# Two buffers for the normalised tile, and a chunk normalised one turn earlier in the halo loop of a state-space and ternary-FFN kernel

## The reference, cut to what matters

```python
u = jnp.einsum('bld,nd->bln', _layernorm(x), W_in)      # 64 states
h = h * Abar + u_t * Bbar                               # scan over the tokens
x = x + jnp.einsum('bln,dn->bld', h * C, W_out)
...
def _quant_weight(w): s = mean(|w|); wq = clip(round(w / s), -1, 1) * s
def _quant_act(x): scale = 127 / max|x| per row; xq = round(x * scale) / scale
h = gelu(_quant_act(_layernorm(x)) @ _quant_weight(w1).T)   # 1024 -> 4096
x = x + _quant_act(h) @ _quant_weight(w2).T                 # 4096 -> 1024
```

## Time and profile before

| | us |
|---|---|
| runs before | 2258.49, 2260.24 (median), 2263.87 |
| the profiled execution | 2268.22 |
| its span, slowest core (core 4) | 2266.7 |
| spans of the 8 cores | 2242.1 to 2266.7 |
| DVE busy, whole span | 1448.2 (64%) |
| PE busy, whole span | 1275.0 (56%) |
| ACT, POOL busy, whole span | 444.0, 218.4 |

### The profile page before, as it was taken

How to read it: one execution, slowest core, us unless ns; L and a number is a source line. 1 busy time by engine, 2 the same in 40 slices (tenths; PEclk the granted TensorE clock), 3 DMA queues, 4 the chain that set the end, 5 groups by cost and what they waited for, 6 DMA issues and landing times.

```text
span 2266.7 us, 33749 instructions; the slowest of 8 cores (2242.1 to 2266.7 us)
## 1 busy us (share of the span) xinstructions
PE 1275.0 (56%) x12185; PEld 893.0 (39%) x12248; DVE 1448.2 (64%) x2155; ACT 444.0 (20%) x682; POOL 218.4 (10%) x164
## 2 busy tenths in 40 slices
PE   0002222211111126788778887887887787788887
PEld 0001111111111115556545655554565456556553
DVE  3655555544444457767777777777677777777753
ACT  0002222111111013222212221222222122212210
POOL 0000000111111111001100100110010001001000
PEclk9999999999999997989888988988898898889998
DMA  5973343111111100000000100010000001000000
GB/s 142 292 241 120 130 139 130 38 56 37 56 38 47 46 19 20 10 29 29 20 29 11 38 29 10 29 38 11 29 29 20 29 11 38 29 10 29 20 12 27
DMA packets 30825, 120.15 MB, mean 53 GB/s; under 512 B 3972, under 2 KB 3972, under 8 KB 28612
## 3 DMA queue, kind: packets, MB, share of 16 engines
q1 hardware_dynamic: 15428, 56.63, 7.7%
q0 software_dynamic: 9712, 38.28, 4.6%
q10 hardware_dynamic: 5520, 23.07, 3.4%
HBM read 101.19 MB, written 16.78 MB: 52 GB/s over the span
## 4 chain that ended last, share of the span: by engine, by line
DVE 41%; PE 22%; DMA 15%; issue 8%; DVEq 4%; ACT 4%; POOLq 4%; ACTq 0%; SPq 0%; POOL 0%
PE pout L821 13%; DVE hred L631 10%; DMA vs<-w 5%; DVE TLblk L571 3%; DMA xbT<-xo 3%; DMA xbT<-xh 3%; POOLq L249 3%; DVE xn L588 2%; DMA k<-w 2%; ACT xnfm L355 2%; DVE TLblk L604 2%; DVE vs L565 2%; PE pmisc L795 2%; DVE x L504 2%; DVE TLblk L574 1%
## 5 line engine op out<-in xcount | busy, mean ns | idle before, releaser
L821 PE MATMUL pout<-t2T,k 128*128 128x512 bf16 x1985 | 513.2, 421 | 9.6 <-DVEq L536 4.1
L821 PEld LDWEIGHTS pout<-t2T,k 128*128 128x128 bf16 x2048 | 215.5, 107 | 292.2 <-issue 106.6
L765 PE MATMUL pm1b<-k1fm,t1T 128*128 128x128 bf16 x4096 | 289.3, 237 | 72.4 <-ACTq L336 72.4
L765 PEld LDWEIGHTS pm1b<-k1fm,t1T 128*128 128x128 bf16 x4096 | 271.4, 107 | 76.8 <-issue 76.8
L765 PE MATMUL pm1a<-k1fm,t1T 128*128 128x128 bf16 x4096 | 253.2, 221 | 0.0
L654 DVE TENSOR_TENSOR vs<-h_sb,sc2bc 128x1024 f32<-128x1024 f32 x128 | 156.9, 1225 | 147.3 <-ACTq L365 75.6
L631 DVE TENSOR_REDUCE hred<-h_sb 128x128 f32<-128x4096 f32 x32 | 227.2, 7099 | 28.2 <-ACTq L336 22.4
L765 PEld LDWEIGHTS pm1a<-k1fm,t1T 128*128 128x128 bf16 x4096 | 236.1, 99 | 3.4 <-issue 0.3
L785 PE MATMUL pT<-identb,xn 128*128 128x128 bf16 x512 | 53.5, 268 | 297.3 <-DVEq L590 297.3
L726 PE MATMUL pT<-identb,k 128*128 128x128 bf16 x512 | 64.7, 305 | 199.9 <-DVEq L508 199.9
L785 PEld LDWEIGHTS pT<-identb,xn 128*128 128x128 bf16 x512 | 42.7, 120 | 312.2 <-issue 305.6
(11 more groups left out here) (153 smaller groups left out, 1258.0 us busy)
## 6 DMA issues: line engine op xcount, KB each, us to landing
xbT<-xh SPq DMA_DIRECT2D x16, 1024.0 KB, 4.9
xbT<-xo SPq DMA_DIRECT2D x16, 1024.0 KB, 4.9
out<-out_s POOLq DMA_DIRECT2D x32, 512.0 KB, 3.0
h_sb<-w SPq DMA_DIRECT2D x11, 1024.0 KB, 7.7
vs<-w ACTq DMA_DIRECT2D x11, 1024.0 KB, 7.2
vs<-w ACTq DMA_DIRECT2D x22, 512.0 KB, 4.2
h_sb<-w SPq DMA_DIRECT2D x21, 512.0 KB, 3.7
k<-w POOLq DMA_DIRECT2D x10, 1024.0 KB, 7.7
```

The source lines that it names most:

```text
L765: ti = t.matmul(reg, t1T[:, k * 4096 + m * 128:k * 4096 + (m + 1) * 128], k1fm[oi % 2][:, k * 128:(k + 1) * 128], start=(k == 0), stop=(k ...
L821: ti = t.matmul(pout[:, d * 512:(d + 1) * 512], k2[:, hk * 128:(hk + 1) * 128], t2T[:, hk * 1024 + d * 512:hk * 1024 + d * 512 + 512], sta ...
```

## The change

`xn` becomes two buffers, taken by chunk parity, and `xnfm` becomes one, so SBUF use stays as it is. The waits follow: `ve_fa2(it)` now waits for the transposes of chunk it-2, and `se_xnfm(it)` for the matmuls of chunk it-1. In the halo turns (b from 0 to 30) the DVE now runs all of `ve_fa1a`, `ve_fa1b`, `ve_fa2` of chunk b+2 ahead of `ve_uev` and `ve_scan` of chunk b+1; from b = 31 on its order is the old one. The lists of PE, ACT, POOL and SP keep their order.

```diff
-    xn = sbt("xn", (128, D), BF16)
-    xnfm = [sbt(f"xnfm{i}", (128, D), BF16) for i in range(2)]
+    xn0 = sbt("xn_0", (128, D), BF16)
+    xn1 = sbt("xn_1", (128, D), BF16)
+    xn = [xn0, xn1]
+    xnfm0 = sbt("xnfm0", (128, D), BF16)
+    xnfm = [xnfm0, xnfm0]
...
             def se_xnfm(it):
                 s.wait_ge(S["xnT"], it + 1)
-                if it >= 2:
-                    s.wait_ge(S["umm"], it - 1)
+                if it >= 1:
+                    s.wait_ge(S["umm"], it)
...
             def ve_fa2(it):
                 v.wait_ge(S["sqr1a"], it + 1)
-                if it >= 1:
-                    v.wait_ge(S["xnT"], it)
+                if it >= 2:
+                    v.wait_ge(S["xnT"], it - 1)
...
-                v.tensor_scalar(xn[:], xb[it % 2][:], TL["inv"][:, 0:1],
+                v.tensor_scalar(xn[it % 2][:], xb[it % 2][:], TL["inv"][:, 0:1],
...
             for b in range(NIT + 3):
                 oi1 = b - NCH - 1
                 oi3 = b - NCH - 3
+                halo = b < NCH - 1
+                if halo and b + 2 < NIT:
+                    ve_fa1a(b + 2)
+                    ve_fa1b(b + 2)
+                    ve_fa2(b + 2)
                 if b + 1 < NIT:
                     ve_uev(b + 1)
                     ve_scan(b + 1)
...
-                if b + 2 < NIT:
+                if not halo and b + 2 < NIT:
                     ve_fa1a(b + 2)
                     ve_fa1b(b + 2)
                 if NCH <= b + 1 < NIT:
                     ve_fb2(b + 1)
-                if b + 2 < NIT:
+                if not halo and b + 2 < NIT:
                     ve_fa2(b + 2)
...
-                                     xn[:, f * 128:(f + 1) * 128], identb[:])
+                                     xn[it % 2][:, f * 128:(f + 1) * 128],
+                                     identb[:])
```

More of the change, by code:

```diff
@@ L659, in ve_back_a @@
                 D_().then_inc(S["k2_"], 1)
[L661 to L666, removed]
+            for _it0 in range(2):
+                ve_fa1a(_it0)
+                ve_fa1b(_it0)
+                ve_fa2(_it0)
             ve_uev(0)
```

## The result

Eight runs of each kernel: 2262.05 us before (median), 2207.06 us after. The ratio is 0.976, 95% interval 0.974 to 0.978: 2.4% faster. The forecast was 2205.6 us, in a range of 2196 to 2222. In some executions, most of experiment 4's among them, the cores of one die had a lower granted clock (0.86 to 0.91 against 0.92 to 0.93) and took longer; the medians count all executions and the ratios leave out the slowest of these, so the two can differ a little. The profiled execution of the changed kernel took 2203.03 us.

The account below looks back on a forecast made before the run. In the halo no engine was full; a chain of waits set the pace, chiefly the DVE's for PE's u, with the load beside it. Median 2260.2 less 15 x 3.64 = 54.6 us gives 2205.6; range 2196 to 2222.

Parts of the forecast that it names:

- The buffers: Two `xn` and one `xnfm`: no gain or loss, as the old and new waits are met anyway.
- The order, odd chunks: Halo, after the even `xn`: u is ready, so 3.64 us saved in each of 15 odd chunks, 54.6 us.
- the count of 15: Halo chunks 2 to 32 move, 15 of them odd; chunk 32's u again starts 3.87 us after its `xn`.
- The order, even chunks: Halo, after the odd `xn`: idle time moves from L624 (3.87 us) to L565's load wait (about 3.7), gain 0.
- What is late next: Halo, ACT: the odd chunk's root stands behind the even chunk's copy, with 2.4 us of slack.
- The load: Halo load in shorter rounds: median 4.9 us taken; 4.8 would give 1.6 us, 8.0 would cost 50.
- The shared port: Two-input DVE operations and POOL's square exclude each other for a whole instruction; the halo's scan stays clear, sum unchanged.
- Main stage and clock: Main stage begins 55 us sooner and lasts as before; clock could give 6 us either way, taken as 0.
- the load wins by a hair: Halo, after the odd `xn`: chain with scan frees the DVE at 5.0 us, the load lets L565 start at 5.10.
- my forecast for experiment 4: Second copy in the kernel before: 1.1 us per odd and 0.3 per even chunk, about 22 us, 2284, ratio 1.010.

Follow-up runs that it names:

- experiment 4: Kernel before, with ACT copying the transposed tile to `xnfm` twice in chunks 0 to 31: 2313.46 us, ratio 1.022.
- Experiments 1 and 2: First, changed kernel with the old buffers and waits: 2210.49 us, ratio 0.978. Second, kernel before with only the new buffers and waits: 2257.48 us, ratio 1.0005.
- Experiment 3: Changed kernel, with ACT copying the transposed tile to `xnfm` twice in chunks 0 to 31: 2205.97 us, ratio 0.976.
- Experiment 5: Changed kernel with the halo's loads split, one 512 KB load for each chunk: 2161.24 us, ratio 0.954.
- experiment 6: Kernel before with the halo's loads split, one 512 KB load for each chunk: 2267.2 us, ratio 1.003.
- experiment 8: Changed kernel with the halo's loads split and its small DVE steps written with one tensor input: 2120.12 us, ratio 0.936.
- experiment 7: Changed kernel with all loads split, one for each chunk in halo and main stage: 2149.81 us, ratio 0.950.

## Why the prediction was right

**The buffers: nothing.** Experiments 1 and 2 show it: the halo keeps its length to within 2 us with or without them, in either order.

**The order, odd chunks: 15 x 3.64 us.** The gap between the even `xn` and the odd L568 is 1.33 us instead of 5.01. The gap before L627 came out at 0.20 us, not 0.24; with it the sum is 15 x 3.68 = 55.2 us, and 55.3 us is what the halo lost. At the end chunk 32's u came 3.87 us after its `xn` (at 723.63), as the count of 15 needs. Experiment 3 shows that the chain is no longer on the path, experiment 4 that it was.

**The order, even chunks: 0.** The wait moved from L624 to L568, 4.0 us a round (3.7 were said). Experiment 5 shows that this wait was real idle time, and experiment 6 that it was no bound in the old order.

**What is late next.** L350 never stood behind ACT's copy, and with 1.1 us more there it still did not.

**The load.** It landed in 4.75 to 5.27 us in the chain's pieces, where it was 4.82 to 5.24 in the kernel before; the shorter rounds did not stretch it.

**The shared port.** No scan met a square in the changed halo. The Trainium skill, SBUF — State Buffer, "SBUF: two separate sides", names as excluded, beside operations with two SBUF inputs, those in a 2-port mode; L615 in experiment 8 (1.54 us under the square against 0.81) would fit that, but no trace shows in which mode it ran. The rule's "whole instruction" is too strong for these traces: L615 ended 0.55 us after the square and the scan of experiment 4 0.27 us after it, though alone they take 0.81 and 0.48 us, so a part of each was done under the square (by the profile's times, of which POOL's are rough).

**Main stage and clock.** 1352.5 us against 1351.4, with a granted clock of 0.88: the 0 that I took was right.

**Where the trace was read too thinly.** The prediction says "the load wins by a hair" after an odd chunk, and leaves it there. Behind that hair stood the square, which starts at the landing and holds up a scan that has not started by then. The change moves the scan's start from 0.85 to 4.5 us ahead of it (473.52 and 478.00), so the sum does not need it; my forecast for experiment 4 did, and missed by 17 us in the halo (39 against 22).

## What to carry to other kernels

Where two waits run side by side and end within a few tenths of each other, taking one away gains nothing there; count the places where only one of them stands, and give the gain for these alone. A reordering on one engine's list can take out a latency that is spread over three others, and needs no new buffer if the old wait is met anyway. When a chain is gone, look at what the wait has moved to: here splitting a load that was harmless before (and whose splitting cost 0.3% in the old order) gave almost as much again. And where an edit takes a wait away and adds a stall elsewhere, as in the main stage of experiment 7, a time that stays the same says nothing of either alone; count both in the trace.

## What the runs showed of the hardware

A 1.89 us square on POOL stretched a DVE step on 128 x 1 elements from 0.16 to 1.72 us, a scan on 64 x 128 from 0.48 to 1.83, and the normalising `tensor_scalar` (float32 to bfloat16, 1024 elements a partition) from 0.81 to 1.54 us; they ended 0.01, 0.27 and 0.55 us after the square. A small step that began 0.11 us before the square ran in its 0.16 us. The row sum with an accumulator (L568) took 1.22 us with or without the square. The same small step with one tensor and a per-partition scalar takes 0.21 us and runs under the square.
